# Perceiver layer on one core: the attention stage's matmuls as pairs on 64-row halves of the array

## The chip, the cores and the metric

One core of a Trainium2 chip runs the whole layer in one launch. The metric is device time in microseconds (us) of that launch, lower is better. TensorE (PE) does the matmuls, and each matmul has a weight load of its own (PEld in the profile) that overlaps other matmuls. VectorE (DVE), ScalarE (ACT) and GpSimd (POOL) work beside it; SyncE (SP) issues all transfers.

## The reference

Only the cross attention matters here. For each of 32 batches, with 64 query tokens, 16 heads and 1601 context tokens of 192 channels:

```
q = query @ w_q
k, v = split(context @ w_kv)
scores = einsum('bhqd,bhkd->bhqk', q, k) * SCALE
attn = softmax(scores, axis=-1)
out = einsum('bhqk,bhkd->bhqd', attn, v)
```

The kernel doesn't form `k` and `v`. It folds the key weights into the queries, so that the scores are a product of (heads x queries) by 192 channels with the 192 x 1601 context; it multiplies the probabilities with the raw context (1601 x 192), and applies the value weights in a later stage. A wkv recurrence and a feed-forward part follow; nothing in them changes.

All products are made of split operands. A number is a high part (rounded to fp32r) plus a low part (the rest), and a product is hi x hi + lo x hi + hi x lo.

## The kernel before

Four stages follow each other: `project_queries`, `attend`, `attention_output`, `mix_and_feed`. Only `attend` is touched. It makes 256 **steps**, 8 for each batch; a step is 128 rows of (head, query) against the 1601 context tokens (1602 with padding, `CW`). Two batches (16 steps) are one pass of a loop: the first and the last pass are written out, 14 passes are the loop's.

In step j, TensorE computes

- the **scores** (`step_scores`, L725): 192 channels are 128 (a) and 64 (b). The b block lies twice in a 128-row tile, its high part in rows 0 to 63 and its low part in rows 64 to 127, and the b block of the queries lies twice too. So five matmuls of 128 rows make one piece of the scores: q_hi x ct_a, q_lo x ct_a, q_hi x ct_lo, and for b q_hi and q_lo against the stacked tile. The 1602 columns are cut into pieces of 288, 512, 512 and 290 (`CHUNKS`), each in a PSUM bank of its own: 20 matmuls in a step.
- the **product** of step j - 4 (`product`, L741 and L743; `LAG` is 4): 13 tiles of 128 context tokens, for each a matmul of the high probabilities with [context_hi | context_lo] (384 columns) and one of the low probabilities with context_hi (192 columns), both added up in one PSUM bank of `acc` (two of these take turns): 26 matmuls.

Around it in each step:

- VectorE takes the row maximum of each half of the scores (L672 after `left_ready`, L674 after `scores_ready`), joins them (L677), adds the two halves of an earlier product (`out`, L653) and transposes the sum (L659); then it waits for the exponentials, transposes 1664 columns of probabilities (L683), and makes the row sum and its reciprocal (L684, L686). It runs in this order, and nothing on it passes anything else.
- ScalarE rounds the transposed probabilities of step j - 4 to their high part (L569, two instructions; waits for the product before, since `pt_hi` is one buffer), scales one half of a product (`half_out`, L560), does one piece of the next batch's operands, and then the two exponentials (L601), which wait for the maximum.
- GpSimd makes the low part of the probabilities (L505, two instructions, for tiles 0 to 5 and 6 to 12), then a piece of the next batch's operands (L513, L517, L524 or L532).
- SyncE moves the transposed probabilities across partitions (`move`) and loads the next batch.

The order is written out by hand. The scores of a step may start when the exponentials of the step before have read the banks (`exp_left`, `exp_done`), the product's two parts when `pt_lo_done` says that their tiles are there.

## Time and profile before

| | |
|---|---|
| median of 3 runs | 2585.05 us (2583.1 to 2589.5) |
| profiled execution | 2584.14 us, its span 2582.3 us |
| PE busy | 2348.9 us (91%), 13872 matmuls |
| PE weight loads busy | 2139.0 us (83%) |
| DVE, ACT, POOL busy | 1709.3, 1516.8, 1702.8 us |
| first and last product matmul of `attend` | start 214.7 and 2112.5 us |

Busy time of PE is modelled and pipelined matmuls overlap in it. What a matmul costs is therefore read from the distance between the starts of two that follow each other, not from its duration. "idle before ... <- X" is the time that an engine stood before an instruction, and X is what ended it.

### The profile page before, as it was taken

Reading aid. Unit: us, or ns where it says so; the run is one execution under the profiler, and the core shown is the slowest. Engines: PE = TensorE matmul, PEld = TensorE weight load, DVE = VectorE, ACT = ScalarE, POOL = GpSimd, SP = SyncE. Lnnn points to the kernel's source line nnn. Section 1 sums busy time; section 2 is a strip of 40 time slices with the busy share of each in tenths; the row PEclk is TensorE's granted clock in tenths of the full one; section 3 lists DMA queues with packets and bytes.
Section 4 is the critical chain, followed back from the end, with each engine's and each line's share of the span. In section 5 each row is a group of like instructions: output and inputs, shape, how many; then the busy total and the mean of one; then the engine's idle time right before and its main releaser. Section 6 shows DMA issues by size and latency. Waiting matters only on the chain. (4 is left out here: it accounts for less than half of the span.)

```text
span 2582.3 us, 43038 instructions
## 1 busy us (share of the span) xinstructions
PE 2348.9 (91%) x13872; PEld 2139.0 (83%) x13872; DVE 1709.3 (66%) x2663; ACT 1516.8 (59%) x2456; POOL 1702.8 (66%) x874
## 2 busy tenths in 40 slices
PE   5948999999999999999999999999999957855777
PEld 3637999999999999999999999999999955744666
DVE  7746666666666666666666666666666626768772
ACT  4645666666666666666666666666666525543442
POOL 1015888888888888888888888888888632022553
PEclk9979999999999999999999999999999978986888
DMA  4767778887877888888878877887888549910000
GB/s 133 227 188 172 194 192 196 196 200 194 192 192 194 193 196 198 194 196 198 198 193 193 194 193 192 198 197 193 196 199 196 136 103 221 195 49 0 9 9 17
DMA packets 387683, 434.18 MB, mean 168 GB/s; under 512 B 45701, under 2 KB 362281, under 8 KB 387625
## 3 DMA queue, kind: packets, MB, share of 16 engines
q1 hardware_dynamic: 387624, 433.45, 69.2%
q8 instruction: 32, 0.52, 0.1%
q14 instruction: 27, 0.21, 0.0%
HBM read 162.73 MB, written 52.43 MB: 83 GB/s over the span
## 5 line engine op out<-in xcount | busy, mean ns | idle before, releaser
L505 POOL TENSOR_TENSOR p_pt_lo<-p_landed,p_pt_hi 128x768 fp32r<-128x768 f32 (+1 forms) x512 | 1005.7, 1986 | 359.8 <-ACT p_pt_hi L569 359.8
L741 PE MATMUL p_acc<-p_nat,p_pt_hi 128*128 128x384 f32 x3328 | 975.8, 361 | 14.4 <-POOL p_pt_lo L505 14.0
L743 PE MATMUL p_acc<-p_nat,p_pt_lo 128*128 128x192 f32 x3328 | 844.6, 254 | 0.0
L601 ACT ACTIVATE p_prob<-p_scores,p_negmax 128x800 f32<-128x800 f32 (+1 forms) x512 | 471.6, 927 | 512.3 <-DVE p_negmax L677 512.3
L725 PE MATMUL p_scores<-p_ct_hi,p_q_hi 128*128 128x512 f32 (+2 forms) x2048 | 709.7, 350 | 39.3 <-DVE p_ct_hi L701 27.2
L725 PE MATMUL p_scores<-p_ct_hi,p_q_lo 128*128 128x512 f32 (+2 forms) x2048 | 703.6, 347 | 0.0
L683 DVE STREAM_TRANSPOSE p_turned<-p_prob 128x1664 f32<-128x1664 f32 x256 | 489.4, 1912 | 317.5 <-ACT p_prob L601 317.5
L741 PEld LDWEIGHTS p_acc<-p_nat,p_pt_hi 128*128 128x128 f32 x3328 | 629.2, 189 | 17.2 <-issue 14.9
L743 PEld LDWEIGHTS p_acc<-p_nat,p_pt_lo 128*128 128x128 f32 x3328 | 639.2, 192 | 0.0
L569 ACT ACTIVATE p_pt_hi<-p_landed 128x768 fp32r<-128x768 f32 (+1 forms) x512 | 432.3, 892 | 159.2 <-PE p_acc L743 152.4
L725 PEld LDWEIGHTS p_scores<-p_ct_hi,p_q_hi 128*128 128x128 f32 x2048 | 387.6, 189 | 87.7 <-issue 28.0
L725 PEld LDWEIGHTS p_scores<-p_ct_hi,p_q_lo 128*128 128x128 f32 x2048 | 389.6, 190 | 44.3
L674 DVE TENSOR_REDUCE p_halfmax<-p_scores 128x1 f32<-128x801 f32 x256 | 254.1, 993 | 210.8 <-PE p_scores L725 210.6
L725 PE MATMUL p_scores<-p_ct_lo,p_q_hi 128*128 128x512 f32 (+2 forms) x1024 | 353.2, 345 | 0.0
L672 DVE TENSOR_REDUCE p_halfmax<-p_scores 128x1 f32<-128x800 f32 x256 | 253.8, 991 | 59.6 <-PE p_scores L725 52.7
L725 PEld LDWEIGHTS p_scores<-p_ct_lo,p_q_hi 128*128 128x128 f32 x1024 | 193.9, 189 | 22.0
L532 POOL TENSOR_TENSOR p_nat<-p_raw,p_nat 128x1152 fp32r<-128x1152 f32 (+1 forms) x62 | 178.7, 2882 | 0.0
L517 POOL TENSOR_TENSOR p_q_lo<-p_stage,p_q_hi 128x1024 fp32r<-128x1024 f32 x62 | 148.4, 2394 | 12.7 <-ACT p_q_hi L579 12.7
L653 DVE SCALAR_TENSOR_TENSOR p_o_q<-p_acc,p_rinv,p_part 128x192 f32<-128x192 f32 x256 | 107.0, 418 | 32.8 <-ACT p_part L560 31.8
L513 POOL TENSOR_TENSOR p_ct_lo<-p_stage,p_ct_hi 128x802 fp32r<-128x802 f32 (+1 forms) x62 | 111.0, 1790 | 25.4 <-ACT p_ct_hi L576 25.4
L560 ACT ACTIVATE p_part<-p_acc,p_rinv 128x192 f32<-128x192 f32 x256 | 103.1, 403 | 28.8 <-PE p_acc L743 28.8
L524 POOL TENSOR_TENSOR p_ct_hi<-p_stage,p_ct_hi 64x802 fp32r<-64x802 f32 (+1 forms) x62 | 108.8, 1755 | 5.3
(191 smaller groups left out, 2646.8 us busy)
## 6 DMA issues: line engine op xcount, KB each, us to landing
p_landed<-p_turned SPq DMA_DIRECT2D x2048, 104.0 KB, 2.2
p_raw<-in_ctx SPq DMA_DIRECT2D x96, 312.0 KB
o_scratch<-p_o_t SPq DMA_DIRECT2D x256, 96.0 KB, 2.6
qk_scratch<-p_out_a SPq DMA_DIRECT2D x16, 1024.0 KB, 4.6
p_oa<-o_scratch SPq DMA_DIRECT2D x32, 512.0 KB, 6.1
p_stage<-qk_scratch SPq DMA_DIRECT2D x31, 512.0 KB, 3.9
p_stage<-qk_scratch SPq DMA_DIRECT2D x62, 256.0 KB, 4.3
p_stage<-in_ctxT SPq DMA_DIRECT2D x31, 401.0 KB, 3.3
```

What stands on the lines that cost most here:

```text
L505: nc.gpsimd.tensor_tensor(pt_lo[:, t0:t1, :, :], by_tile(slot, t0, t1), bits(pt_hi[:, t0:t1, :, :]), ALU.subtract).then_inc(pt_lo_done, 1)
L513: nc.gpsimd.tensor_tensor(ct_lo[1 - par][:, lo:hi], stage[:, u, 0:hi - lo], bits(ct_hi[1 - par][:, 0, lo:hi]), ALU.subtract).then_inc(ct_a ...
L517: nc.gpsimd.tensor_tensor(stepped(q_lo[1 - par][:, u - 3, :]), by_step(stage[:, u - 3, :]), bits(stepped(q_hi[1 - par][:, u - 3, :])), ALU ...
L532: nc.gpsimd.tensor_tensor(x[:, t0:t1, DC:2 * DC], raw[:, t0:t1, :], bits(x[:, t0:t1, 0:DC]), ALU.subtract).then_inc(nat_done, 1)
L569: nc.scalar.activation(pt_hi[:, t0:t1, :, :], by_tile(slot, t0, t1), ACT.Copy).then_inc(pt_hi_done, 1)
L601: nc.scalar.activation(prob[:, lo:hi], scores[:, S0 + lo:S0 + hi], ACT.Exp, bias=negmax[:, par:par + 1], accum_out=rowsum[:, par, h:h + 1] ...
L672: nc.vector.tensor_reduce(halfmax[:, par, 0:1], scores[:, S0:S0 + MID], AX.X, ALU.max, negate=True).then_inc(halfmax_done, 1)
L674: nc.vector.tensor_reduce(halfmax[:, par, 1:2], scores[:, S0 + MID:S0 + NKV], AX.X, ALU.max, negate=True).then_inc(halfmax_done, 1)
L683: nc.vector.transpose(turned[:, j % 4, :], prob[:, :]).then_inc(turned_done, 1)
L725: last = nc.tensor.matmul(scores[:, S0 + lo:S0 + hi], w, x, start=m == 0, stop=m == len(terms) - 1)
L741: nc.tensor.matmul(acc[k % 2][:, 0:2 * DC], pt_hi[:, t, :, :].rearrange("p i x -> p (i x)"), x[:, t, :], start=t == 0, stop=False, skip_gr ...
L743: last = nc.tensor.matmul(acc[k % 2][:, 0:DC], pt_lo[:, t, :, :].rearrange("p i x -> p (i x)"), x[:, t, 0:DC], start=False, stop=t == KT - ...
```

## The change

Every matmul of `attend` is cut into two of 64 rows, one on rows 0 to 63 of the array (`UPPER`) and one on rows 64 to 127 (`LOWER`), issued one after the other and writing to different PSUM banks.

- Scores: the pieces are 400, 400, 400 and 402 columns. For each half h of the scores, five pairs go first ("own": upper rows on the even piece, lower rows on the odd one), for both halves; then four pairs with the pieces swapped. The low part of b times q_lo is the term that is left out in the swap, so each row half makes nine passes. 36 matmuls in a step instead of 20.
- The low part of b lies in the lower rows for even pieces and in the upper rows for odd ones (`ROWS_B`), so GpSimd makes it in four instructions of a batch (L530 of the changed kernel), not two.
- `left_ready` comes after both halves' own pairs and the first half's swapped ones.
- Product: upper and lower rows add up in two banks; 52 matmuls in a step instead of 26. `acc` is two pairs of banks.
- VectorE adds the four parts (two banks, high and low column half) in one reduction over 768 elements to 192 (`sum_out`, L664), placed at the start of its step; ScalarE scales the sum (`scale_out`), and VectorE transposes it at the old place (`turn_out`).

```diff
-    CHALF = [(0, 802), (802, CW)]
-    EDGE = (CW - 2 * 512) // 4 * 2
-    CHUNKS = [(0, EDGE), (EDGE, EDGE + 512), (EDGE + 512, EDGE + 1024), (EDGE + 1024, CW)]
-    S0 = 512 - EDGE
-    MID = EDGE + 512
+    C = 400
+    CHUNKS = [(0, C), (C, 2 * C), (2 * C, 3 * C), (3 * C, CW)]
+    CHALF = [(0, 2 * C), (2 * C, CW)]
+    MID = 2 * C
+    PLACE = [512 - C, 512, 3 * 512 - C, 3 * 512]
+    UPPER, LOWER = slice(0, DCB), slice(DCB, P)
+
+    ROWS_B = [(UPPER, LOWER), (LOWER, UPPER)]
...
-                    dst = ct_hi[1 - par][DCB:P, 1, lo:hi]
-                    nc.gpsimd.tensor_tensor(dst, stage[DCB:P, u - 6, 0:hi - lo], bits(dst), ALU.subtract).then_inc(ct_b_done, 1)
-                    pool.wait_ge(ct_b_done, n * 2 + (u - 3))
+                    for c in (2 * (u - 6), 2 * (u - 6) + 1):
+                        (c0, c1), rows = CHUNKS[c], ROWS_B[c % 2][1]
+                        dst = ct_hi[1 - par][rows, 1, c0:c1]
+                        nc.gpsimd.tensor_tensor(dst, stage[rows, u - 6, c0 - lo:c1 - lo], bits(dst), ALU.subtract).then_inc(ct_b_done, 1)
+                    pool.wait_ge(ct_b_done, n * 4 + (2 * u - 6))
...
+            def sum_out(r, j, first):
...
+                dve.wait_ge(acc_ready, p + 1)
+                if not (first and k == 0):
+
+                    dve.wait_ge(o_scaled, p)
+                parts = acc[k % 2][:, :, 0:2 * DC].rearrange("p b (h c) -> p c b h", c=DC)
+                nc.vector.tensor_reduce(o_sum[:, :], parts, AX.XY, ALU.add).then_inc(acc_read, 1)
...
-                q = lambda t, k: t[par][:, k, (j % SB) * P:(j % SB + 1) * P]
-                for c, (lo, hi) in enumerate(CHUNKS):
-                    if c % 2 == 0 and not (first and j == 0):
-
-                        pe.wait_ge(exp_left if c == 0 else exp_done, s)
-                    ct_a, ct_b, ct_al = (t[:, lo:hi] for t in (ct_hi[par][:, 0, :], ct_hi[par][:, 1, :], ct_lo[par]))
-                    terms = ((q(q_hi, 0), ct_a), (q(q_lo, 0), ct_a), (q(q_hi, 0), ct_al), (q(q_hi, 1), ct_b), (q(q_lo, 1), ct_b))
-                    for m, (w, x) in enumerate(terms):
-                        last = nc.tensor.matmul(scores[:, S0 + lo:S0 + hi], w, x, start=m == 0, stop=m == len(terms) - 1)
-                    if c == 1:
-                        last.then_inc(left_ready, 1)
-                last.then_inc(scores_ready, 1)
+                def passes_of(chunk_pair, count, own):
+
+                    for m in range(count):
+                        w, x = terms[m]
+                        for rows, c in zip((UPPER, LOWER), chunk_pair):
+                            lo, hi = CHUNKS[c]
+                            last = nc.tensor.matmul(scores[:, PLACE[c]:PLACE[c] + hi - lo], w[rows], x[rows, lo:hi], start=own and m == 0,
+                                                    stop=not own and m == count - 1, skip_group_check=True)
+                    return last
+
+
+                for h in range(2):
+                    if not (first and j == 0):
+
+                        pe.wait_ge(exp_done if h else exp_left, s)
+                    passes_of((2 * h, 2 * h + 1), len(terms), True).then_inc(own_done, 1)
+                for h in range(2):
+                    pe.wait_ge(own_done, s * 2 + (h + 1))
+                    passes_of((2 * h + 1, 2 * h), len(terms) - 1, False).then_inc(scores_ready if h else left_ready, 1)
...
-                        nc.tensor.matmul(acc[k % 2][:, 0:2 * DC], pt_hi[:, t, :, :].rearrange("p i x -> p (i x)"), x[:, t, :], start=t == 0, stop=False,
-                                         skip_group_check=True)
-                        last = nc.tensor.matmul(acc[k % 2][:, 0:DC], pt_lo[:, t, :, :].rearrange("p i x -> p (i x)"), x[:, t, 0:DC], start=False,
-                                                stop=t == KT - 1, skip_group_check=True)
+                        for w, width in ((pt_hi, 2 * DC), (pt_lo, DC)):
+                            for i, rows in enumerate((UPPER, LOWER)):
+                                last = nc.tensor.matmul(acc[k % 2][:, i, 0:width], w[rows, t, :, :].rearrange("p i x -> p (i x)"),
+                                                        x[rows, t, 0:width], start=t == 0 and w is pt_hi, stop=t == KT - 1 and w is pt_lo,
+                                                        skip_group_check=True)
```

VectorE's instructions of one step inside the loop, before. `p_halfmax`, `p_negmax` are the maxima, `p_o_q` and `p_o_t` the product's output, `p_turned` the transposed probabilities.

```order
L683 STREAM_TRANSPOSE p_turned<-p_prob 128x1664 [waits p2_moved1,p2_exp_done]
L684 TENSOR_REDUCE p_rowtot<-p_rowsum 128x1
L686 RECIPROCAL p_rinv<-p_rowtot 128x1 [waits p2_rowtot_done]
L671 REGISTER_ALU
L672 TENSOR_REDUCE p_halfmax<-p_scores 128x1 [waits p2_left_ready]
L674 TENSOR_REDUCE p_halfmax<-p_scores 128x1 [waits p2_scores_ready]
L676 ISA
L677 TENSOR_REDUCE p_negmax<-p_halfmax 128x1 [waits p2_halfmax_done]
L649 REGISTER_ALU
L653 SCALAR_TENSOR_TENSOR p_o_q<-p_acc,p_rinv,p_part 128x192 [waits p2_o_done,p2_part_done]
L659 STREAM_TRANSPOSE p_o_t<-p_o_q 128x6x32 [waits p2_acc_read]
```

The same step after the change:

```order
L692 STREAM_TRANSPOSE p_turned<-p_prob 128x1664 [waits p2_moved1,p2_exp_done]
L693 TENSOR_REDUCE p_rowtot<-p_rowsum 128x1
L695 RECIPROCAL p_rinv<-p_rowtot 128x1 [waits p2_rowtot_done]
L659 REGISTER_ALU
L664 TENSOR_REDUCE p_o_sum<-p_acc 128x192 [waits p2_o_scaled,p2_acc_ready]
L680 REGISTER_ALU
L681 TENSOR_REDUCE p_halfmax<-p_scores 128x1 [waits p2_left_ready]
L683 TENSOR_REDUCE p_halfmax<-p_scores 128x1 [waits p2_scores_ready]
L685 ISA
L686 TENSOR_REDUCE p_negmax<-p_halfmax 128x1 [waits p2_halfmax_done]
L675 STREAM_TRANSPOSE p_o_t<-p_o_q 128x6x32 [waits p2_o_scaled]
```

The reading of `p_acc` has moved from behind the joined maximum, where it took two of the three operands of an addition, to the place between the reciprocal and the first maximum, and it reads all four parts.

TensorE's scores of one step inside the loop, before, up to the second bank (the two later pieces read alike, the third behind a wait for `p2_exp_done`):

```order
L725 MATMUL p_scores<-p_ct_hi,p_q_hi 128x288 [waits p2_exp_left]
L725 MATMUL p_scores<-p_ct_hi,p_q_lo 128x288
L725 MATMUL p_scores<-p_ct_lo,p_q_hi 128x288
L725 MATMUL p_scores<-p_ct_hi,p_q_hi 128x288
L725 MATMUL p_scores<-p_ct_hi,p_q_lo 128x288
L725 MATMUL p_scores<-p_ct_hi,p_q_hi 128x512
```

And after, the end of the second half's own pairs and the first half's swapped ones, up to the second half's (x2 is a pair of equal width):

```order
L738 MATMUL p_scores<-p_ct_hi,p_q_lo 128x400
L738 MATMUL p_scores<-p_ct_hi,p_q_lo 128x402
L749 ISA
L738 MATMUL p_scores<-p_ct_hi,p_q_hi 128x400 [waits p2_own_done]
L738 MATMUL p_scores<-p_ct_hi,p_q_hi 128x400
L738 MATMUL p_scores<-p_ct_hi,p_q_lo 128x400 x2
L738 MATMUL p_scores<-p_ct_lo,p_q_hi 128x400 x2
L738 MATMUL p_scores<-p_ct_hi,p_q_hi 128x400 x2
L749 REGISTER_ALU
L738 MATMUL p_scores<-p_ct_hi,p_q_hi 128x402 [waits p2_own_done]
```

Each piece was finished before the next began; now the first half of the scores is finished only four pairs before the whole.

## Rows read from the trace of the kernel before

**Rows 1.** Windows: us, busy time (instructions) of each engine, granted PE clock, DMA

```profile
1000.00:1400.00 400.00, 400.00 (x2493) 376.33 (x2491) 270.20 (x433) 261.10 (x433) 329.61 (x164) 1.00 0.80 194
```

**Rows 2.** Waits from 600 to 1400 us: us in total, times, longest

```profile
DVE p_turned L683 <- ACT p_prob L601: 133.3, 109, 1.3
DVE p_halfmax L674 <- PE p_scores L725: 89.7, 108, 0.8
...
DVE p_halfmax L672 <- PE p_scores L725: 20.0, 82, 0.4
```

**Rows 3.** Timeline of one step on PE: start us, duration us, engine, line

```profile
1300.27 0.32 PE L725 MATMUL p_scores<-p_ct_hi,p_q_hi 128*128 128x288 f32 x1
...
1300.96 0.39 PE L725 MATMUL p_scores<-p_ct_hi,p_q_hi 128*128 128x512 f32 x1
...
1303.27 0.30 PE L725 MATMUL p_scores<-p_ct_hi,p_q_hi 128*128 128x290 f32 x1
...
1303.95 0.34 PE L741 MATMUL p_acc<-p_nat,p_pt_hi 128*128 128x384 f32 x1
...
1307.65 0.36 PE L725 MATMUL p_scores<-p_ct_hi,p_q_hi 128*128 128x288 f32 x1
```

**Rows 4.** Timeline of DVE and ACT in the same step

```profile
1304.15 0.99 DVE L674 TENSOR_REDUCE p_halfmax<-p_scores 128x1 f32<-128x801 f32 x1 [0.83 <-PE p_scores L725]
...
1305.18 0.15 DVE L677 TENSOR_REDUCE p_negmax<-p_halfmax 128x1 f32<-128x2 f32 x1
...
1305.37 0.93 ACT L601 ACTIVATE p_prob<-p_scores,p_negmax 128x800 f32<-128x800 f32 x1 [2.08 <-DVE p_negmax L677]
...
1306.29 0.93 ACT L601 ACTIVATE p_prob<-p_scores,p_negmax 128x801 f32<-128x801 f32 x1
...
1307.33 1.91 DVE L683 STREAM_TRANSPOSE p_turned<-p_prob 128x1664 f32<-128x1664 f32 x1 [1.24 <-ACT p_prob L601]
```

**Rows 5.** Timeline of DVE in a step where L672 waited for nothing

```profile
1314.84 1.91 DVE L683 STREAM_TRANSPOSE p_turned<-p_prob 128x1664 f32<-128x1664 f32 x1 [1.34 <-ACT p_prob L601]
...
1316.82 0.17 DVE L686 RECIPROCAL p_rinv<-p_rowtot 128x1 f32<-128x1 f32 x1
1317.12 0.99 DVE L672 TENSOR_REDUCE p_halfmax<-p_scores 128x1 f32<-128x800 f32 x1
```

**Rows 6.** Timeline of ACT and POOL: high and low part of the probabilities

```profile
1300.53 1.69 ACT L569 ACTIVATE p_pt_hi<-p_landed 128x768 fp32r<-128x768 f32 x2 [0.62 <-PE p_acc L743]
...
1301.46 3.93 POOL L505 TENSOR_TENSOR p_pt_lo<-p_landed,p_pt_hi 128x768 fp32r<-128x768 f32 x2 [1.76 <-ACT p_pt_hi L569]
```

**Rows 7.** Groups of weight loads in `project_queries`, 128 and 64 columns

```profile
L266 PEld LDWEIGHTS p_ap<-p_stack,p_wks_lo 128*128 128x128 f32 x64 | 12.1, 188 | 1.4
...
L268 PEld LDWEIGHTS p_bp<-p_stack,p_wks_lo 128*64 128x64 f32 x64 | 8.6, 134 | 6.2
```

**Rows 8.** Timeline of PE in `mix_and_feed`, where a 33-row matmul stands between full ones

```profile
2404.44 0.28 PE L1431 MATMUL p_yp<-p_w_lo,p_hid_hi 128*128 128x256 f32 x1
2404.56 0.28 PE L1431 MATMUL p_yp<-p_w_hi,p_hid_lo 128*128 128x256 f32 x1
2404.77 0.38 PE L1431 MATMUL p_yp<-p_bias,p_ones 33*128 33x256 f32 x1
2405.08 0.38 PE L1431 MATMUL p_yp<-p_w_hi,p_hid_hi 128*128 128x256 f32 x1
```

**Rows 9.** Groups of DVE and ACT from 600 to 1400 us: product's output, longest piece of a next batch

```profile
L653 DVE SCALAR_TENSOR_TENSOR p_o_q<-p_acc,p_rinv,p_part 128x192 f32<-128x192 f32 x108 | 45.1, 418 | 0.5
L560 ACT ACTIVATE p_part<-p_acc,p_rinv 128x192 f32<-128x192 f32 x109 | 43.9, 402 | 0.0
...
L592 ACT ACTIVATE p_nat<-p_raw 128x1344 fp32r<-128x1344 f32 x14 | 18.4, 1315 | 0.0
```

**Rows 10.** DMA: the instruction queue of PE's program; issues, median us to landing

```profile
q8 instruction: 32, 0.52, 0.1%
...
p_landed<-p_turned SPq DMA_DIRECT2D x2048, 104.0 KB, 2.2
```

More of the change, by code:

```diff
@@ L350, in attend @@
         scores = pb("scores", [P, 2048])
-        acc = [pb(f"acc{i}", [P, 512]) for i in range(2)]
+        acc = [pb(f"acc{i}", [P, 2, 512]) for i in range(2)]
         raw_in = sem("raw_in")
@@ L605, in drain @@
                 if not (first and j < LAG + 1):
-                    half_out(r * SPP + (j - LAG - 1), (j - LAG - 1) % SB, (j - LAG - 1) % 2, first and j == LAG + 1)
+                    scale_out(r * SPP + (j - LAG - 1), (j - LAG - 1) % SB, first and j == LAG + 1)
             def raise_high(r, j, first):
@@ L646, in _, with turn_out @@
         def _(dve):
[L647 to L661 removed]
+            def sum_out(r, j, first):
+                if first and j < LAG + 1:
+                    return
+                k = j - LAG - 1
+                p = r * SPP + k
+                dve.wait_ge(acc_ready, p + 1)
[3 more added lines that the diff above has]
+                nc.vector.tensor_reduce(o_sum[:, :], parts, AX.XY, ALU.add).then_inc(acc_read, 1)
+            def turn_out(r, j, first):
                 if first and j < LAG + 1:
@@ L665, in drain @@
                 ring, batch = k % SB, k // SB
-                fresh = ring % (SB // 2) != 0 or (first and batch == 0)
-                out(r * SPP + k, ring, k % 2, None if fresh else (r * SPB + batch) * (16 * G), first and k == 0)
+                dve.wait_ge(o_scaled, r * SPP + (k + 1))
+                if ring % (SB // 2) == 0 and not (first and batch == 0):
+                    dve.wait_ge(stored[ring // (SB // 2)], (r * SPB + batch) * (16 * G))
+                nc.vector.transpose(o_t[:, :, ring, :], o_q[:, :].rearrange("p (k x) -> p k x", x=R)).then_inc(o_done, 1)
             def step(r, j, first):
                 s, par = r * SPP + j, j % 2
+                sum_out(r, j, first)
                 dve.wait_ge(left_ready, s + 1)
-                nc.vector.tensor_reduce(halfmax[:, par, 0:1], scores[:, S0:S0 + MID], AX.X, ALU.max, negate=True).then_inc(halfmax_done, 1)
+                nc.vector.tensor_reduce(halfmax[:, par, 0:1], scores[:, PLACE[0]:PLACE[0] + MID], AX.X, ALU.max, negate=True).then_inc(halfmax_done, 1)
                 dve.wait_ge(scores_ready, s + 1)
-                nc.vector.tensor_reduce(halfmax[:, par, 1:2], scores[:, S0 + MID:S0 + NKV], AX.X, ALU.max,
+                nc.vector.tensor_reduce(halfmax[:, par, 1:2], scores[:, PLACE[2]:PLACE[2] + NKV - MID], AX.X, ALU.max,
                                         negate=True).then_inc(halfmax_done, 1)
@@ L705, in _ @@
             for j in range(LAG + 1):
-                drain(NB // SPB, j, False)
+                sum_out(NB // SPB, j, False)
+                turn_out(NB // SPB, j, False)
         @block.tensor
```

46 lines of the change are left out of this document (20 added, 26 removed).

## The prediction

> **What bounds the kernel now.** I read the windows first, to see which engine is full. In 400 us TensorE is busy all of it at a granted clock of 1.00 (its 2.4 GHz level) and runs 2493 matmuls; at 46 a step that is 54.2 steps, 7.38 us each [rows 1]. So TensorE sets the step. The timeline gives its parts: scores 3.68 us (1300.27 to 1303.95), product 3.70 us (to 1307.65) [rows 3]. By distance between starts, 288 columns cost 138 ns, 290 cost 136, 512 cost 231 ((1303.27 - 1300.96) / 10), and a product tile of 384 + 192 columns 285 ns (3.70 / 13). At 2.4 GHz 512 columns are 213 ns and 576 are 240 ns, so each matmul carries 15 to 20 ns beyond its columns, and a tile 45.
>
> Next the waits, to see how far behind the others are. VectorE is in a ring with ScalarE: maxima, exponentials, transpose, next maxima, each after the other. In it VectorE waits for TensorE's scores 89.7/108 = 0.83 us a step before the second maximum and 20.0/109 = 0.18 us before the first [rows 2]. Its wait of 1.22 us for the exponentials [rows 2] is inside the ring, no slack. So the ring alone would take 7.38 - 0.83 - 0.18 = 6.37 us. By its pieces, start to start: transpose to reciprocal 1.98 and to the first maximum 0.30 [rows 5], first maximum 0.99, second to the joined one 1.03, to the exponential 0.19, to the second one 0.92, to the transpose 1.04 [rows 4, 5]: 6.45. The two differ by 0.08, by which an instruction can start ahead of the end of the one before.
>
> A third ring goes through `pt_hi`: ScalarE starts it 0.26 us after a product's end (1300.27, then 1300.53), GpSimd follows 0.93 later and needs 3.93 for both parts [rows 3, 6], then TensorE does the last seven tiles, 7 x 0.285 = 2.0. That is 7.12 us, only 0.26 below today's step.
>
> **The change, part by part.** *Scores.* 20 matmuls become 18 pairs of 400 (a few 402) columns. If the two halves of the array stream at the same time, a pair costs what one matmul of 400 columns does: between 137 and 231 ns, 184 by the columns, so 18 x 0.184 = 3.31 us instead of 3.68. *Product.* The same columns in each half: 3.70 us as before, if the halves' loads overlap too. TensorE's own step: 7.01 us.
>
> No row of this trace shows two matmuls on different rows at once, so I bound it. From below: the above. From above: nothing runs at once, 36 x 0.184 + 2 x 3.70 = 14.0 us. Between them lies the weight load. One of 64 columns lasts 134 ns, one of 128 lasts 188 [rows 7]: 0.84 ns a column, 107 ns for 128 columns. The number of loads goes from 46 to 88. If loads of the two halves go one after the other, a pair of scores takes 2 x 107 = 214 ns and a tile 4 x 107 = 428: 3.85 + 5.56 = 9.41 us. I take the lower bound, since both halves' loads and streams use different partitions; that is the main assumption. The Trainium skill (TensorEngine Tiling (Array Packing), Key Properties) says that tiles on different rows can load and multiply in parallel; no run here shows it yet. It says as well (TensorE: Matmul & The Clock Gate, LDWEIGHTS) that a load's time goes by its columns, not its rows; rows 7 agree on the columns, and with loads in single file this rule gives the 9.41 us.
>
> *One mode throughout.* A 33-row matmul between full ones starts 0.21 us after the one ahead where 0.12 is usual, and the full one behind it 0.31 after it [rows 8]: 0.28 us lost for going over and back. In `attend` everything is 64 rows now, so this is paid once, under 1 us.
>
> *`sum_out`.* A reduction of 768 elements from PSUM: 800 take 0.99 and 2 take 0.15 [rows 4, 5], so 1.05 ns an element, 0.96 us; with the 0.08 of overlap 0.88. It stands between the reciprocal and the first maximum, so it is in the ring. The 0.42 us addition that goes away [rows 9], and the small transpose, lay in VectorE's wait for the exponentials and give nothing back. Ring: 6.37 + 0.88 = 7.25 up to 6.45 + 0.96 = 7.41 us; I take 6.37 + 0.92 = 7.29.
>
> *Is more late in it?* Count from the transpose's start. `sum_out` runs from 2.28 to 3.2; TensorE's first half is ready about 0.25 us after 10 + 4 pairs, 2.6 + 0.25 = 2.9 after its start, which is before 0; no wait. ScalarE then scales (0.4 us, as the instruction it replaces), ends at 3.6, and does a piece of the next batch, at most 1.32 (both [rows 9]), so it is free at 5.0; the exponential wants it at 5.3. Cover 0.3 us; were it gone, it would cost what is over, in one step of eight. `pt_hi` starts at about 0.05, its low part is done at 4.9, the product's second part ends at 7.0, inside 7.29. *GpSimd's extra instructions* (four of half width for two) follow its low part in two steps of eight and lie before the next batch starts; nothing, or some 0.2 us a batch (6 us in all) if that cover is gone.
>
> *Sum.* 7.38 - 7.29 = 0.09 us a step (-0.03 to 0.13), for the 252 steps in which scores and product stand together: 23 us (-8 to 33). Head and tail: under 1 us.
>
> *The loop.* Before, the queue that brings instructions made 32 packets, 0.52 MB, for the whole execution [rows 10], although the loop's body ran 14 times: nothing was fetched twice. The body's TensorE instructions nearly double. If a jump back must fetch again, it may cost one transfer, 2.2 us [rows 10], or nothing where TensorE had work queued: 0 to 14 x 2.2 = 31 us. I take 0.5 a pass, 7 us. The Trainium skill (Runtime: NRT & Kernel Launch, Instruction fetch mechanics) gives TensorE room for 2048 instructions, and says that a jump out of what is held fetches by DMA; with load and matmul counted apart the body goes from about 1470 to 2820, so by it this fetch comes.
>
> 2584.1 - 23 + 7 = 2568 us against the profiled execution's own time. The median of the runs is 0.9 us above that execution, which changes nothing here.
>
> **Rivals.**
>
> 1. *Loads in single file.* 9.41 us a step: 252 x 2.03 = +512, 3096 us. For it: 107 ns a load is what the tiles already show, since the low matmul's 192 columns (80 ns) don't cover it. Against: different partitions. 13%.
> 2. *Each matmul pays its own 15 ns.* If the 15 ns that a matmul has beyond its columns is paid by the array's single queue, a pair costs 167 + 30 and a tile about 285 + 30: 3.55 + 4.10 = 7.65 us, +0.27 x 252 = +68, with the loop some 2655 us. TensorE is then the bound again, from 7.3 us on. This one ends on the other side. 17%, anywhere in 2600 to 2720.
> 3. *Nothing runs at once*: +6.6 x 252, 4250 us. 4%.
> 4. *VectorE pays less than I think*, so that the ring through `pt_hi` decides: 7.12 to 7.2 us, 252 x 0.22 = 55 less, 2530 to 2550 us. 9%.
> 5. *The fetch at the jump is paid in full* or twice over, with the ring as forecast: 2592 to 2620 us. 7%.
> 6. *As forecast*: 2550 to 2590 us. 50%.
>
> **How the numbers follow.** Less or more than 0.3% (8 us) of 2585 is what can be told: faster is under 2577, slower over 2593. Faster: case 4 and 0.34 of case 6, 0.43. Same: the rest of case 6, 0.16. Slower: the others, 0.41. The likeliest case gives 2568, with 2550 to 2590 as its own range. The range over the cases is 2535 to 2700: it leaves out 1 and 3 (0.17) and the ends of 2 and 4.
>
> **What would show it.** Right: a step of 7.25 to 7.35 us; the second of a pair starts within some ns of the first, pairs 184 ns apart, tiles 285; VectorE no longer waits for scores (1.01 us before), `sum_out` 0.9 to 1.0 us; TensorE now idles, about 0.3 us a step, before the product's second part (for GpSimd) or the scores; more packets in the instruction queue. Wrong: pairs 214 or 368 ns apart; a tile over 310 ns; a granted clock below 1.00; ScalarE's exponential waiting for ScalarE's own queue; TensorE idle for over 2 us at each jump.

## The result, and the profile after

The changed kernel takes 2723.07 us (median of 4 runs, 2712.91 to 2728.42) against 2587.28 us before (4 runs, 2583.1 to 2589.85): ratio 1.0523, with the interval 1.0493 to 1.0552. It is 136 us slower, outside the range of the prediction. The profiled execution of the changed kernel took 2727.83 us, its span is 2726.0 us.

The ordinary step came out as long as forecast. This is the timeline of PE in one undisturbed step (start us, duration us; x2 is a pair, both halves in one row):

```profile
1300.29 0.40 PE L738 MATMUL p_scores<-p_ct_hi,p_q_hi 64*128 64x400 f32 x2
1300.49 0.38 PE L738 MATMUL p_scores<-p_ct_hi,p_q_lo 64*128 64x400 f32 x2
...
1303.60 0.36 PE L765 MATMUL p_acc<-p_nat,p_pt_hi 64*128 64x384 f32 x2
1303.78 0.28 PE L765 MATMUL p_acc<-p_nat,p_pt_lo 64*128 64x192 f32 x2
1303.86 0.38 PE L765 MATMUL p_acc<-p_nat,p_pt_hi 64*128 64x384 f32 x2
...
1305.48 0.45 PE L765 MATMUL p_acc<-p_nat,p_pt_hi 64*128 64x384 f32 x2
...
1307.57 0.36 PE L738 MATMUL p_scores<-p_ct_hi,p_q_hi 64*128 64x400 f32 x2
```

Scores take 3.31 us (3.68 in [rows 3]), 18 pairs at 184 ns; a product tile 288 ns; the step 7.28. The small wait ahead of 1305.48 (0.47 instead of 0.29 behind the tile before) is the one for GpSimd's low part, and it is what sets the step. ScalarE, GpSimd and VectorE beside it:

```profile
1300.58 1.69 ACT L575 ACTIVATE p_pt_hi<-p_landed 128x768 fp32r<-128x768 f32 x2 [2.19 <-PE p_acc L765]
1301.50 3.92 POOL L509 TENSOR_TENSOR p_pt_lo<-p_landed,p_pt_hi 128x768 fp32r<-128x768 f32 x2 [1.08 <-ACT p_pt_hi L575]
...
1307.17 1.91 DVE L692 STREAM_TRANSPOSE p_turned<-p_prob 128x1664 f32<-128x1664 f32 x1 [1.67 <-ACT p_prob L607]
...
1310.35 0.99 DVE L681 TENSOR_REDUCE p_halfmax<-p_scores 128x1 f32<-128x800 f32 x1 [0.16 <-PE p_scores L738]
...
1314.43 1.91 DVE L692 STREAM_TRANSPOSE p_turned<-p_prob 128x1664 f32<-128x1664 f32 x1 [1.71 <-ACT p_prob L607]
```

The ring through `pt_hi` closes: 0.29 us from the scores' start to the high part, 0.92 to the low part, 3.92 for both its instructions, 0.06 to the seventh tile, 2.09 to the next scores, 7.28 in all. In each of the 117 steps of the loop that have no delay in them, the seventh tile starts 0.05 us behind the end of the low part. VectorE meanwhile goes from transpose to transpose in 7.26 us and waits 0.16 of it for TensorE, so its own ring would take 7.10.

The groups of the page agree: `sum_out` (L664) is as long as estimated, and ScalarE's scaling (L566) a little longer than what it replaces [rows 9]. Total busy us, mean ns, idle before:

```profile
L664 DVE TENSOR_REDUCE p_o_sum<-p_acc 128x192 f32<-128x768 f32 x256 | 244.8, 956 | 41.7 <-PE p_acc L765 35.1
...
L566 ACT ACTIVATE p_o_q<-p_o_sum,p_rinv 128x192 f32<-128x192 f32 x256 | 115.5, 451 | 134.5 <-DVE p_o_sum L664 134.1
```

But TensorE is no longer busy all the time. The window that answers to [rows 1]:

```profile
1000.00:1400.00 400.00, 372.39 (x4352) 355.00 (x4350) 264.39 (x396) 243.54 (x396) 302.58 (x162) 0.96 0.74 180
```

TensorE stands idle 28 of 400 us, and its granted clock is 0.96, not 1.00. The waits from 600 to 1400 us, which answer to [rows 2]:

```profile
DVE p_turned L692 <- ACT p_prob L607: 172.7, 100, 2.0
...
DVE p_halfmax L681 <- PE p_scores L738: 83.2, 77, 8.8
...
ACT p_pt_hi L575 <- DMA p_landed<-p_turned: 67.1, 36, 3.3
...
PE p_scores L738 <- issue: 32.1, 12, 3.6
...
DVE p_halfmax L683 <- PE p_scores L738: 1.6, 5, 0.3
```

VectorE's wait before the second maximum is gone (1.6 us in all where [rows 2] have 89.7), as forecast; but it still waits for TensorE before the first one, 77 times. New are three things: TensorE waits 12 times for nothing that the profile shows (`issue`; a fetch of instructions would be shown so) ahead of scores; VectorE now and then waits up to 8.8 us for scores; and ScalarE waits 36 times for a landed transfer. The instruction queue and the transfers, against [rows 10]:

```profile
q8 instruction: 230, 3.77, 0.6%
...
p_landed<-p_turned SPq DMA_DIRECT2D x2048, 104.0 KB, 2.6
```

230 packets instead of 32.

To see where these waits fall I took the start of every step's scores from the timeline and put the distances in columns by the step's place in a pass of 16, medians over the passes of the loop, in us (the last column is the mean of the loop's passes without the first and the last):

```
place in pass    0     1    2    3    4    5    6    7    8    9   10   11   12   13   14    15   pass of 16
before         7.43 7.38 7.38 7.38 7.38 7.38 7.38 7.38 7.41 7.39 7.39 7.39 7.39 7.39 7.39  7.39   118.2
after         12.74 7.21 7.21 7.21 7.36 7.30 8.78 7.27 7.95 7.27 7.28 7.28 7.95 7.29 8.01 10.20   128.5
```

Over the 250 distances the stage goes from 1850.1 to 1986.2 us, +136.1, and this divides into four: the ordinary step, median 7.386 before and 7.287 after, -25; the places 15 and 0 of the 13 passes with a jump back behind them, +106; 65 other steps that are over 0.2 us late, nearly all at even places, +57; the rest -3. So there are two losses to explain: a **seam** of 106/13 = 8.2 us at each jump, and **late even steps**, 57 us.

One seam of the changed kernel, first the timeline of PE, then windows around it (us, PE busy (instructions), granted clock, DMA share, GB/s):

```profile
933.62 0.25 PE L765 MATMUL p_acc<-p_nat,p_pt_lo 64*128 64x192 f32 x2
936.62 0.70 PE L738 MATMUL p_scores<-p_ct_hi,p_q_hi 64*128 64x400 f32 x2 [2.75 <-issue]
...
937.43 0.55 PE L738 MATMUL p_scores<-p_ct_lo,p_q_hi 64*128 64x400 f32 x2
941.54 0.70 PE L738 MATMUL p_scores<-p_ct_hi,p_q_hi 64*128 64x400 f32 x2 [3.55 <-issue]
...
942.37 0.54 PE L738 MATMUL p_scores<-p_ct_hi,p_q_hi 64*128 64x400 f32 x2
942.70 0.54 PE L738 MATMUL p_scores<-p_ct_hi,p_q_lo 64*128 64x400 f32 x2
```

```profile
929.00:936.00 7.00, 4.87 (x62) 1.00 0.66 167
936.00:942.00 6.00, 1.83 (x8) 0.56 0.88 204
942.00:947.00 5.00, 5.00 (x34) 0.51 0.69 166
947.00:956.00 9.00, 9.00 (x118) 1.00 0.41 117
```

TensorE waits 2.75 us for its first scores, does three pairs, waits 3.55 us again; instruction packets start at 930.94, 933.8 and 938.77. Behind this pause the granted clock is 0.51 to 0.56, its 1.2 GHz level, and pairs are 0.33 us apart instead of 0.184: 18 pairs x 0.15 = 2.7 us on top of 6.3. From 600 to 2000 us, which hold 11 jumps, there are 139 such slow pairs, 139 x 0.15 = 21 us or 1.9 a jump; before there was none. The two waits come to 5.8 us on average over all 13 jumps, so that waits and slow pairs make 7.7 of the 8.2.

### The profile page after: what moved, and what is told of

Read it like the earlier page. It is cut to its first block and busy times, and to the rows that moved or that the text cites. A ratio compares the mean times of both kernels' runs of the same rounds, so it can differ in the third digit from the quotient of the medians.

```text
span 2726.0 us, 65054 instructions
## 1 busy us (share of the span) xinstructions
PE 2371.8 (87%) x24624; PEld 2191.3 (80%) x24624; DVE 1801.5 (66%) x2666; ACT 1544.7 (57%) x2456; POOL 1712.1 (63%) x936
## 5 line engine op out<-in xcount | busy, mean ns | idle before, releaser
L765 PE MATMUL p_acc<-p_nat,p_pt_hi 64*128 64x384 f32 x6656 | 1026.7, 367 | 65.0 <-POOL p_pt_lo L509 59.8
L765 PE MATMUL p_acc<-p_nat,p_pt_lo 64*128 64x192 f32 x6656 | 875.5, 251 | 0.0
L738 PE MATMUL p_scores<-p_ct_hi,p_q_hi 64*128 64x400 f32 (+1 forms) x4096 | 709.0, 356 | 112.3 <-issue 70.9
L765 PEld LDWEIGHTS p_acc<-p_nat,p_pt_hi 64*128 64x128 f32 x6656 | 663.5, 186 | 140.8 <-issue 90.7
L765 PEld LDWEIGHTS p_acc<-p_nat,p_pt_lo 64*128 64x128 f32 x6656 | 671.8, 189 | 0.0
L738 PE MATMUL p_scores<-p_ct_hi,p_q_lo 64*128 64x400 f32 (+1 forms) x3072 | 559.6, 351 | 0.0
L738 PEld LDWEIGHTS p_scores<-p_ct_hi,p_q_hi 64*128 64x128 f32 x4096 | 413.7, 191 | 123.6 <-issue 109.0
L738 PE MATMUL p_scores<-p_ct_lo,p_q_hi 64*128 64x400 f32 (+1 forms) x2048 | 371.7, 350 | 0.0
L738 PEld LDWEIGHTS p_scores<-p_ct_hi,p_q_lo 64*128 64x128 f32 x3072 | 316.8, 193 | 0.0
L664 DVE TENSOR_REDUCE p_o_sum<-p_acc 128x192 f32<-128x768 f32 x256 | 244.8, 956 | 41.7 <-PE p_acc L765 35.1
L566 ACT ACTIVATE p_o_q<-p_o_sum,p_rinv 128x192 f32<-128x192 f32 x256 | 115.5, 451 | 134.5 <-DVE p_o_sum L664 134.1
L530 POOL TENSOR_TENSOR p_ct_hi<-p_stage,p_ct_hi 64x400 fp32r<-64x400 f32 x124 | 110.5, 891 | 9.9
```

The costliest lines, as they stand in the source:

```text
L664: nc.vector.tensor_reduce(o_sum[:, :], parts, AX.XY, ALU.add).then_inc(acc_read, 1)
L738: last = nc.tensor.matmul(scores[:, PLACE[c]:PLACE[c] + hi - lo], w[rows], x[rows, lo:hi], start=own and m == 0, stop=not own and m == cou ...
L765: last = nc.tensor.matmul(acc[k % 2][:, i, 0:width], w[rows, t, :, :].rearrange("p i x -> p (i x)"), x[rows, t, 0:width], start=t == 0 and ...
```

## The experiments

### First: the seam

In x1_hint, x2_slot and x6_hint_slot TensorE's loop alone is written out with an option of the loop. The first announces the jump back ahead of it, which is meant to let the instructions at its target be fetched early:

```
-            passes(pe, body)
+            body(0, True, False)
+            only = bass.OrderedEngineSet([pe.engine])
+            with nc.Fori(1, NB // SPB - 1, engines=only, hint_back_edge=True) as r:
+                body(r, False, False)
+            body(NB // SPB - 1, False, True)
```

> The changed kernel with one instruction more: at the top of each pass TensorE's sequencer is told that the jump back will be taken. Theory J (the loop's body no longer fits where TensorE's instructions are held, each jump back waits for two fetches): 14 passes have 13 jumps, the steps round a jump took 2.9 and 5.5 us more than 7.27; at least the first wait goes, so 13 x 2.9 = 38 us less, and if the hint covers both, 13 x 8.4 = 109 us less: 2615 to 2685 us, packets in the instruction queue still about 230. Theory B (it is the batch boundary: operands that GpSimd finishes late, now in four instructions instead of two): nothing changes, 2723 us, and the 8 us stay at the pass's seam. Theory Q (a pair of matmuls is slower than forecast somewhere): nothing changes.

Measured: 2660.82 us, 1.0261 (1.0228 to 1.0294), 205 instruction packets. Places 14, 15 and 0 take 9.35, 7.48 and 7.18 us, and there is not one slow pair of scores. Places 15 and 0 together have lost all but 3 of their 106 us. The kernel gains only 62 (68 by the two ratios), because the late steps rise from 57 to 93 us. 12 of these 36 lie at place 4 and 21 at place 14. With the seam gone SyncE has less time to catch up (its gaps of over 0.35 us fall from 3.8 to 1.7 us a batch), which can explain place 4. It doesn't explain place 14: x2_slot below keeps a wait at place 15 and the 3.8 us of gaps, and is late there too (40 us, where the changed kernel has 12 and x1_hint 33). Why is open.

x2_slot puts the loop's first instruction at the start of one of the blocks in which instructions are fetched (`head_slot={pe.engine: 0}` in place of the hint), x6_hint_slot has both.

> The changed kernel with the loop's first instruction placed at the start of a fetched block of instructions, nothing else. Theory J: after a jump the block that holds the target is used in full, so the second wait (5.5 us in step 0, because the block was used only in part and the next was fetched after it) falls to about 0.5 or nothing, while the first (2.9 us) stays: 13 x 5 = 65 us less, 2650 to 2670 us. Theory B or Q: 2723 us, no change.

> The changed kernel with both the hint and the loop's head at a block's start. Theory J: both waits at the jump are covered, so it comes to what the version without a loop has, 1.021 of the kernel before (2648 us beside 2593), and no lower, since the fetches and their effect on SyncE stay. Rival: the two don't add up, and it stays at the hint's 1.026.

x2_slot: 2690.23 us, 1.0375 (1.0336 to 1.0413), 217 packets; place 0 falls to 8.56, but 14 and 15 take 10.2 each. So of the two waits the second goes and the first stays, as expected; the seam falls from 106 to 52 us, and the late steps rise to 84. x6_hint_slot: 2662.03 us, 1.029 (1.0262 to 1.0318), no different from x1_hint. A better place of the head is worth 33 us (38 by the ratios), but nothing beside the hint.

x3_unrolled has no jump at all, in the changed kernel; x5_before_unrolled is the same edit on the kernel before; and x4_before_long makes the body of before twice as long, 32 steps:

```
-            passes(pe, body)
+            for r in range(NB // SPB):
+                body(r, r == 0, r == NB // SPB - 1)
```

```
+            body(0, True, False)
+            with pe.Fori(0, (NB // SPB - 2) // 2) as t:
+                for i in range(2):
+                    body(t * 2 + (i + 1), False, False)
+            body(NB // SPB - 1, False, True)
```

> The changed kernel with TensorE's 16 passes written out, no loop; the other engines keep theirs. Theory J: no jump, so 13 x 8.4 = 109 us less, about 2612 us. The blocks are still fetched (about 190 in all), so the second part of the loss stays: each fetch holds back one transfer that SyncE issues by 0.9 us, and steps 6, 8, 12 and 14 of a pass stay 0.7 to 1.5 us late. If they are gone here too, that second part hung on the jumps. Theory B: the seam keeps its 8 us, 2723 us.

> The kernel before with one thing changed: TensorE's loop body holds two passes (32 steps, some 3050 instructions with loads counted apart) and runs 7 times instead of 14. Same matmuls, same order. Theory J: the body no longer fits, 6 jumps at up to 8.4 us cost 20 to 50 us (2605 to 2635 us), the instruction queue goes from 32 packets to over 100, and SyncE's issues beside a fetch get 0.9 us longer, which has slack here and costs little. Theory B or Q: 2585 us as before, with no dependence on the loop's length.

> The kernel before with TensorE's 16 passes written out: instructions are fetched all the time (about 100 packets), but there is no jump. Theory J2 (fetching as such costs only where SyncE has no slack, since it holds back a transfer's issue by 0.9 us; here SyncE waits about 0.4 us a step): 0 to 5 us more than before, steps still 7.38. Rival F (every fetch stops TensorE itself for some tenths of a us): about 6 fetches a pass, 90 in all, by 0.3 to 0.9 us: 27 to 80 us more.

x3_unrolled: 2648.24 us, 1.0213 (1.0183 to 1.0242), 192 packets. x4_before_long: 2615.72 us, 1.0086 (1.0047 to 1.0124), 122 packets; 9.1 to 9.8 us at place 15 where a jump follows, one wait of 2.0 us at each; places 15 and 0 together cost 3.1 us a jump, not 8.2. x5_before_unrolled: 2607.39 us, 1.0072 (1.005 to 1.0094), 108 packets. So a TensorE program with full rows gets a seam too as soon as its loop's body is too long: with load and matmul counted apart the bodies are 1527 instructions (before, no fetch in the loop), 2881 (after) and twice the 1527 (x4_before_long). And without a seam the changed kernel is still 2.1% behind, 36 us more than the 2612 us expected: its late steps cost 78 us, not 57. x5_before_unrolled came between its two expectations: fetches cost something where no jump is.

### Second: the late steps

x7_hint_shadow tests whether the late steps come from VectorE's new work: `sum_out` moves from ahead of the maxima to the time in which VectorE waits for the exponentials, and its output is scaled and turned one step later. x1_hint is its base.

```
-                sum_out(r, j, first)
                 dve.wait_ge(left_ready, s + 1)
...
                 turn_out(r, j, first)
+                sum_out(r, j, first)
                 dve.wait_ge(exp_done, s + 1)
```

> The changed kernel with the hint, and with VectorE's sum of the four parts moved out of its ring to where it waits for the exponentials (scaled and turned a step later). Theory S (what is left over is SyncE: its issues, stretched by fetches, fill a batch's time, and the probabilities land late in steps 6, 8, 12, 14): the steps between fall from 7.2 to about 7.1, but the late ones take that back, so the total stays within 10 us of the hint alone (1.026 of before). Rival D (VectorE's ring sets the time): 252 x 0.15 = 38 us less than the hint alone, 1.011 of before.

Measured: 2650.74 us, 1.0248 (1.0222 to 1.0274), within 10 us of x1_hint. VectorE has its time back; the waits from 600 to 1400 us, first of x1_hint, then of this kernel:

```profile
DVE p_halfmax L681 <- PE p_scores L738: 43.5, 76, 1.6
```

```profile
DVE p_halfmax L680 <- PE p_scores L739: 149.0, 105, 4.3
```

In every ordinary step it now waits about 1 us for the first scores. Yet the ordinary steps are as long as in x1_hint, 7.25 us on average in both kernels, not some 0.1 less as expected, and the late ones stay. So VectorE's ring isn't what makes a step late, and it isn't what sets the ordinary step either: that is the ring through `pt_hi`. x11_relief_shadow (below) shows the same, 7.28 beside 7.28 in x9_relief.

x8_mixed keeps pairs for the second block of the context's transpose alone; everything else has full rows, so that the body is 1665 instructions:

> A version of the same idea with fewer instructions: the scores' a block and the product stay at 128 rows, only the b block's three terms run as pairs on the two halves (24 matmuls and 18 x 400 columns for the scores, 26 for the product, the output summed as in the kernel before). The loop's body is 1665 instructions with loads counted apart, the changed kernel's 2881 and the one before 1527. Theory J: nothing is fetched twice, the instruction queue has about 34 packets, SyncE's moves take 10.4 us as before, no late steps. TensorE: 3.31 + 3.70 us, and 0.28 for going over to halves and back, 7.29 us a step: 23 us less than before, 0.991. If going over costs nothing in a dense stream, the ring through pt_hi decides at 7.12 to 7.2: 45 to 65 us less, 0.975 to 0.983. If it costs the 0.28 twice: 7.57, 1.018.

Measured: 2634.0 us, 1.0181 (1.0157 to 1.0205), 34 packets. No seam, no late step: at every place the median is 7.56 to 7.59 us. What it pays is another thing, seen on PE's timeline:

```profile
1307.58 0.34 PE L730 MATMUL p_scores<-p_ct_lo,p_q_hi 128*128 128x402 f32 x1
1307.84 0.45 PE L735 MATMUL p_scores<-p_ct_hi,p_q_hi 64*128 64x400 f32 x2
1308.13 0.35 PE L735 MATMUL p_scores<-p_ct_hi,p_q_lo 64*128 64x400 f32 x2
...
1308.69 0.68 PE L735 MATMUL p_scores<-p_ct_hi,p_q_hi 64*128 64x400 f32 x4
1309.29 0.44 PE L756 MATMUL p_acc<-p_nat,p_pt_hi 128*128 128x384 f32 x1
1309.58 0.25 PE L758 MATMUL p_acc<-p_nat,p_pt_lo 128*128 128x192 f32 x1
```

Going over takes 0.26 and 0.29 us where 0.184 is usual, going back 0.29 to the tile's low half where it is 0.20, and the last four matmuls (two pairs) 0.60 where two pairs need 0.37. Together these are 0.50 us a step. That is the cost of changing the row mode, which the full change pays once; the step agrees with the last of the expected cases, 0.28 us twice.

**What is late in a late step.** In x3_unrolled, ScalarE, GpSimd and TensorE (each in a view of its own):

```profile
1067.63 1.69 ACT L575 ACTIVATE p_pt_hi<-p_landed 128x768 fp32r<-128x768 f32 x2 [1.87 <-DMA p_landed<-p_turned]
```

```profile
1068.55 3.91 POOL L509 TENSOR_TENSOR p_pt_lo<-p_landed,p_pt_hi 128x768 fp32r<-128x768 f32 x2 [2.23 <-ACT p_pt_hi L575]
```

```profile
1070.53 0.44 PE L765 MATMUL p_acc<-p_nat,p_pt_hi 64*128 64x384 f32 x2 [0.93 <-POOL p_pt_lo L509]
```

The transfer lands late, so the high part starts late, so the low part, so the product. In that kernel TensorE stands still for more than 0.15 us 43 times from 600 to 1900 us, 39 us in all, each time ahead of a product's first tile and some 0.15 us after the end of a low part, and at no other place. Many of these stalls the waits put under `issue`; by their place they belong to this chain.

Why does it land late? The transfers of a pair of steps, a `move`, are 16 issues of SyncE. In the changed kernel and in x8_mixed, which fetches nothing in its loop (SPq's own timeline):

```profile
1363.87 11.95 SPq L431 DMA_DIRECT2D p_landed<-p_turned  x16
```

```profile
1307.61 10.37 SPq L430 DMA_DIRECT2D p_landed<-p_turned  x16
```

One issue takes 0.60 us of SyncE. From 600 to 2000 us of the changed kernel 113 of them take over 1 us, 1.51 on average, and beside every one of the 113 an instruction packet of TensorE's queue starts, within 0.6 us of the issue's own start (there are 152 packets); in the kernel before there is 1 long issue. Packets of ScalarE's queue do nothing of the kind: 56 in the same stretch of x10_before_relief (below), and no issue over 1 us. The transfer itself isn't slowed: behind the end of its issue it lands after 2.2 to 2.3 us on average in both kernels. Means over the loop's passes without the first and the last, from timelines:

```
                     us of a pass   us of a move   packets, 600 to 2000 us
before                 118.23         10.34            2
after                  128.53         11.55          152
x1_hint                122.78         11.21          137
x3_unrolled            122.07         11.18          127
x5_before_unrolled     119.84         10.77           68
x8_mixed               121.13         10.34            0
x13_slow_sync          123.38         11.71            0
x14_stores             119.41         11.11          130
```

So theory S: each fetch holds back an issue of SyncE by 0.9 us, SyncE had little room, and its moves come late. Theory P: a fetch holds TensorE, and the late moves only go along. Four kernels take 13 of SyncE's issues in each batch away (5 of raw values, 8 stores) and let ScalarE make them: x9_relief and x11_relief_shadow on x3_unrolled without and with the edit of x7_hint_shadow, x10_before_relief on before, x12_before_unrolled_relief on x5_before_unrolled.

```
                         sp.wait_ge(nat_done, n * 2 + 2)
-                        load_raw(n + 1)
...
-                        store(n - 1, 0)
...
-                        store(n - 1, 1)
...
+            SLOTS = {(3, 0): ("l", 0), (3, 1): ("l", 1), (4, 0): ("l", 2), (4, 1): ("l", 3), (4, 2): ("l", 4),
+                     (1, 0): ("s0", 0), (1, 1): ("s0", 1), (2, 0): ("s0", 2), (2, 1): ("s0", 3),
+                     (5, 0): ("s1", 0), (5, 1): ("s1", 1), (5 + 1, 0): ("s1", 2), (5 + 1, 1): ("s1", 3)}
```

> x3_unrolled, and SyncE relieved: the 5 transfers of raw values and the 8 stores of each batch are issued by ScalarE between its pieces, so that SyncE issues the four moves alone (4 x about 12 of 58 us). Theory S (a fetch holds back an issue of SyncE, whose queue was nearly full, so that moves land late and ScalarE's first piece of pt_hi waits for them): the late steps go, all are 7.2 to 7.3 us, and the kernel takes 2560 to 2575 us, ratio 0.990 to 0.996. Theory P (the fetches hold TensorE itself, the late moves are only beside it): ratio as x3_unrolled, 1.02. Between: ScalarE's 13 issues of some 0.6 us a batch come late themselves, steps with them 0.3 to 0.6 us longer, 1.000 to 1.010.

> The kernel before with the same 13 issues moved from SyncE to ScalarE: the control. No fetches, a full TensorE: by theory S and P alike 1.000, within 0.003; if ScalarE's issues cost by themselves, slower, and by how much says what the edit itself costs x9_relief (which has less room for them).

> x9_relief with VectorE's sum_out behind its first maxima's transpose turn, in the wait for ScalarE's exponentials, as in x7_hint_shadow. If the late moves are gone, the next limit is the ring of pt_hi: 7.20 us a step, 2545 to 2555 us, ratio 0.983 to 0.988; if VectorE's ring sets the 7.27 of x9_relief no longer, that difference is 0.07 x 252 = 18 us. By theory P: 1.02, as x3_unrolled and x7_hint_shadow.

> x5_before_unrolled (+19.5 us, fetches with half the rows' instructions) with SyncE relieved in the same way. Theory S: its 19.5 us go, ratio that of x10_before_relief, 1.000 to 1.003. Theory P: they stay, 1.007.

Measured, each against the same runs of before (2588.89 us):

```
x9_relief                   2641.56   1.0201 (1.0168 to 1.0234)
x10_before_relief           2635.05   1.0176 (1.0152 to 1.0199)
x11_relief_shadow           2632.82   1.0160 (1.0129 to 1.0190)
x12_before_unrolled_relief  2636.94   1.0184 (1.0161 to 1.0207)
```

The control, x10_before_relief, did not stay at 1.000: moving the issues costs 46 us by itself. In x10_before_relief places 4 and 12 are 0.9 to 1.1 us late and place 0 1.3. ScalarE's timeline shows two reasons: raw values, now in a queue beside the moves, and a wait at its own jump for its own instructions, as I read its queue's 92 packets where before has 27:

```profile
1276.18 1.69 ACT L563 ACTIVATE p_pt_hi<-p_landed 128x768 fp32r<-128x768 f32 x2 [2.12 <-issue]
...
1306.62 0.85 ACT L563 ACTIVATE p_pt_hi<-p_landed 128x768 fp32r<-128x768 f32 x1 [1.65 <-DMA p_landed<-p_turned]
```

```profile
q14 instruction: 92, 0.75, 0.1%
```

What can be read is the difference: x12_before_unrolled_relief is 2 us above x10_before_relief, where without relief the same unrolling cost 19.5 us, and places 6 and 14, late in x5_before_unrolled (7.61, 7.76), are back at their values in x10_before_relief (7.38, 7.53). In x9_relief places 6, 8 and 14 fall from 8.50, 7.59 and 8.33 to 7.27, 7.22 and 7.55. That speaks for S, but 4 and 12 (8.92, 8.97) eat the gain. Two cleaner kernels followed.

x13_slow_sync slows SyncE without any fetch: in the kernel before, two of the 16 transfers of a move are split in two, the same bytes in 18 issues.

```
+                        split = i < 2 and g == G - 1
+                        for part in (slice(2 * par, 2 * par + 1), slice(2 * par + 1, 2 * par + 2)) if split else (slots,):
+                            dst = landed[g * R:(g + 1) * R, part, i, :, :].rearrange("p s t x -> p s (t x)")
+                            sp.dma_start(dst, turned[i * R:(i + 1) * R, part, g * GK:(g + 1) * GK]).then_inc(moved[par], 16)
```

> The kernel before, its loop kept (nothing fetched), but two of the 16 transfers of each move split in two: the same bytes in 18 issues, so that a move takes 11.6 us in SyncE instead of 10.35, about as much as the fetches stretch it in the changed kernel (11.5 on average). TensorE's steps, loop and program stay. Theory S (a stretched SyncE alone makes steps late): even steps late, ScalarE's pt_hi waits for landed transfers, 10 to 60 us more, ratio 1.004 to 1.023. Theory P (a fetch holds TensorE, and late moves only go along with it): 1.000, within 0.003.

Measured: 2677.2 us, 1.034 (1.0323 to 1.0357), 88 us more, beyond the upper end that S gave (60) and far from P's nothing. SPq's timeline over one batch, then two of the waits from 600 to 1400 us, then the instruction queue:

```profile
1315.91 11.88 SPq L429 DMA_DIRECT2D p_landed<-p_turned  x18
1327.99 2.02 SPq L392 DMA_DIRECT2D p_raw<-in_ctx  x4
1330.20 0.24 SPq L394 DMA_DIRECT2D p_raw<-in_ctx  x1
1330.62 0.55 SPq L406 DMA_DIRECT2D p_stage<-in_ctxT  x1
1331.27 0.54 SPq L407 DMA_DIRECT2D p_stage<-in_ctxT  x1
1332.05 11.76 SPq L429 DMA_DIRECT2D p_landed<-p_turned  x18
1344.00 0.54 SPq L406 DMA_DIRECT2D p_stage<-in_ctxT  x1
```

```profile
ACT p_pt_hi L571 <- DMA p_landed<-p_turned: 62.8, 39, 2.1
...
PEld p_acc L743 <- POOL p_pt_lo L507: 29.7, 68, 0.9
```

```profile
q8 instruction: 32, 0.52, 0.1%
```

SyncE goes from issue to issue with 0.1 to 0.2 us between: it is the bound, 61.7 us a batch. From this its load before follows: 61.7 - 4 x (11.71 - 10.34) = 56.2 us of a batch's 59.1, room for 2.9. Its gaps of over 0.35 us say much the same: 4.2 us a batch before, 1.0 here, 1.7 in x1_hint and x3_unrolled. The split transfers themselves land no later, 2.0 us behind the end of an issue. Only even places are late (8.22, 7.90, 8.59, 8.18, 7.88, 8.69 at 0, 4, 6, 8, 12, 14), as a move serves two steps; it is the pattern of the changed kernel, with a loop that fetches nothing.

x14_stores is x3_unrolled with only the 8 stores of a batch issued by ScalarE, the raw values left with SyncE:

> x3_unrolled with only the 8 stores of a batch issued by ScalarE; the raw values' five transfers, which beside the moves made steps 4 and 12 late in x9_relief and x10_before_relief, go back to SyncE. Theory S: about 5 us of 58 less for SyncE in each batch, steps 6, 8 and 14 near 7.27, total 1.005 or below if ScalarE has room for its issues. If ScalarE's own larger program costs (it is fetched too, 92 packets in x10_before_relief where before had 27): 1.010 to 1.020. Theory P: 1.020, as x3_unrolled.

Measured: 2612.42 us, 1.0082 (1.0066 to 1.0099), 36 us less than x3_unrolled with as many packets (192), and ScalarE's own queue back at 27. The late steps fall from 78 to 47 us. The waits from 600 to 1400 us:

```profile
ACT p_pt_hi L571 <- DMA p_landed<-p_turned: 34.4, 22, 2.6
```

It was 59.7 us in x3_unrolled. This is the best of all kernels with 64 rows throughout, and still slower than before; no kernel here beats the one before. The part of the late steps that is left isn't explained by a mean: 56.2 + 4 x 0.77 for the fetches, less some 4 for the stores, is 55 us against a batch of 58.3, and SyncE's gaps are 6.1 us a batch. By place, 27 us of the 47 lie at 6 and 14 (39 in x3_unrolled), and 15 at 2 and 10, where x3_unrolled has 2 and ScalarE now issues stores. The late time also goes with the number of issues over 1 us in a move: in x3_unrolled the step that it serves is 0.2, 0.7 and 1.3 us late on average with none, one and two of them, in x14_stores 0.2, 0.4 and 0.8. So fetches that meet one move and ScalarE's store issues both look like causes; neither was tried by itself.

## Why the prediction was wrong

- **Pairs and tiles** (18 x 0.184, 13 x 0.285): right. 184 and 288 ns; loads of both halves don't add up. (The second of a pair starts some 40 ns behind the first, not within some ns; by the pairs' distance that costs nothing.) Rivals 1 to 3 are out: the kernel is slower, as they said, but by none of their mechanisms.
- **The ring of VectorE** (7.25 to 7.41, taken 7.29): the number came, 7.287, and the gain of 25 us beside 23 forecast, but by luck. `sum_out` takes 0.956 us, as estimated, yet the ring with it takes 7.10: from the reciprocal to the first maximum it counted 0.30 us [rows 5], and `sum_out` now starts 0.08 behind the reciprocal's start. Taking it out of the ring changed no ordinary step (x7_hint_shadow).
- **The ring through `pt_hi`** (7.12, "inside 7.29"; rival 4) is what sets the step, and was put 0.16 too short: 0.06 us from the low part's end to the tile were left out, and the last seven tiles take 2.09, not 2.0.
- **"The loop"** is the step that failed: "it may cost one transfer, 2.2 us [rows 10], or nothing ... 0 to 14 x 2.2 = 31 us. I take 0.5 a pass, 7 us". It measured 106 us in 13 jumps and 57 us elsewhere, 163 where 7 stood. Three things were missing. A jump makes TensorE wait twice, 6.3 us in the seam shown and 5.8 on average, not once for 2.2. After the pause it runs at its 1.2 GHz level for the scores that follow, 1.9 us a jump (21/11). And the bound was put on jumps alone: fetches in straight code hit SyncE, which no step of the prediction looked at. Its room, 3 to 4 us of 59, could have been read from the gaps in SPq's timeline before.
- **Rival 5**, the fetch "in full or twice over", 2592 to 2620 us at 7%, was the right kind with its size from the same bound; so the range ended at 2700 for another rival's reason, and too low.
- The list of what would show it wrong held two things that came: a clock below 1.00, and TensorE idle for over 2 us at each jump.

The rule that the prediction drew on held where it was put to the test. The Trainium skill (Runtime: NRT & Kernel Launch, Instruction fetch mechanics) says that TensorE holds 2048 instructions and that a taken branch out of what is held waits for its fetch. By that rule, the trace agrees: bodies of 1527 and 1665 fetched nothing, those of 2881 and about 3050 did. The same section says that crossing into the next block in straight code is mostly hidden, and that kernels therefore unroll. Here a measurement differs and decides: hidden for TensorE, which never stood still at one in x3_unrolled, but 108 packets cost x5_before_unrolled 19.5 us, in late even steps; that it is through SyncE is read from x12_before_unrolled_relief, where they cost 2.

Shown are: the seam with its clock (x1_hint, x3_unrolled, x4_before_long), that VectorE's ring doesn't set the step (x7_hint_shadow), and that a SyncE slowed by 1.4 us a move makes even steps late and costs 88 us (x13_slow_sync). That a fetch stretches an issue is seen in timing of the traces only, in all kernels with fetches and in none without; by what means they meet was not tried. What remains open is how the late steps left in x14_stores divide between fetches that meet one move and ScalarE's issues, and why place 14 grows with the hint.

## What to carry to other kernels

When a change multiplies an engine's instructions, count them for the loop's body, load and matmul apart, and look at the instruction queue's packets before and after: if a body that ran from its store no longer does, price every jump from rows of a pause (here 3.1 us in x4_before_long and 8.2 in the changed kernel), with the clock that follows it. Look at every queue's slack, SyncE's issues too, before calling a small delay hidden; 93 to 95% full has no room for a fetch on each move. A forecast number that comes true doesn't show which ring sets a step; take the supposed one's load away and look, as x7_hint_shadow does. And halving the rows to fill the array better doubles instructions for the same columns: here it gave 25 us and took 163.

## What the runs showed of the hardware

- Two 64-row matmuls on the array's halves run at once, the second starting 25 to 54 ns behind the first in the scores at 1300 us: a pair of 400 columns takes 184 ns and a product tile 288 ns, where a tile of full rows takes 285.
- A DMA issue of SyncE beside which an instruction packet of TensorE starts can take 1.51 us instead of 0.60 (113 issues at 152 packets). 56 packets of ScalarE stretched none.
- Two issues more in each move of 16, with the same bytes, cost 88 us where SyncE was 93 to 95% full (x13_slow_sync).
- A pause of 2.75 and 3.55 us was followed by 5 us at a granted clock of 0.51. Single waits can do it too: in x3_unrolled from 600 to 2000 us, three of seven waits over 2 us (2.07, 2.32 and 2.99 us from start to start) were followed by 3.4 us at 0.50 to 0.52, with product tiles 0.53 us apart instead of 0.29; four (2.07, 2.17, 2.39, 2.44 us) were not. By these numbers the three cost some 5 us.
- Announcing the jump back (x1_hint) took 103 us of 106 from the seams, while 36 came back in late even steps.
- Changing between full and 64 rows in a dense stream costs about 0.1 us a time, beside what the first and last pair wait (x8_mixed).
